# Rounded output projection, a fused norm guard and a band mask written one step ahead, in a six-layer local-attention kernel

## The chip, the cores and the metric

The kernel runs on one core of one Trainium2 chip. The metric is device time in microseconds: the median of three runs of the kernel before is 4177.26 us (4172.37 to 4178.75). The engines are named as in the profile: PE (TensorE, with PEld for its weight loads), DVE (VectorE), ACT (ScalarE), POOL (GpSimd) and SP (SyncE, which issues the DMAs).

## The reference

Eight sequences of 512 tokens, 128 channels. Stage 1 is a layer norm and one causal attention with 16 heads of 8 channels. Stage 2, where the change lies, is six layers, each an attention over a local window and a gated feed-forward. The attention of a layer:

```
qkv = shift_tokens(x) @ Wqkv               # 16 heads of 64 channels
q = l2norm(q) * q_scale; k = l2norm(k) * k_scale    # l2norm(t) = t / max(|t|, 1e-12)
q = q*cos*scale + rotate_half(q)*sin*scale ; k = k*cos/scale + rotate_half(k)*sin/scale
# window 32: each query sees its own window and the one before it,
# masked to keys j with j <= i <= j + 32
sim = einsum(q, k) * 8 ; sim = where(mask, -max, sim) ; attn = softmax(sim)
out = einsum(attn, v) @ Wo + x
```

## The kernel before

Activations lie channel by token. In stage 2 a layer is a loop over sequences `s` and eight steps `p` (`steps`, L674): a step works on one quad of heads (four heads, `QUADS = 4`) and one half of the tokens (`TOKS = 256`). The work is pipelined over steps. In step n each engine handles, in an order that is written out by hand:

- projection of q and k of step n (L1222 to L1224, into `proj_ps`), and of one tile of v (L1209 to L1211, into `vy_bank`);
- of step n-1 (`LAG_MIX`): the sum of squares per head (`same_head` matmul, L1198), its guard `max(ss, 1e-24)` on DVE (L1064), and ACT's Ln and Exp (L950, L953), which give the inverse norm;
- of step n-2 (`LAG_NORM`): `write_qk` on DVE (L783), rotated q and k times the inverse norm, one instruction of 1024 columns;
- of step n-3 (`LAG_SCORE`): the band mask (L1167: `ident_b` times `band_b`, bf16, which starts the accumulation in the two `score_bank`s), 128 small score matmuls of 32x32 tiles (L1177), the row maximum on DVE (L1020), the exponentials on ACT (L901, two halves of four), the inverse sums on DVE (L1027) and the normalising on POOL (L811);
- of step n-4 (`LAG_VALUE`): the transposes (L1157, into `tr_bank`), their copies on ACT and DVE (L891, L1047), the value products (L1246, 128x64 tiles, into `vy_bank`) and ACT's copy `y` (L943);
- of step n-5 (`LAG_WO`): the output projection in fp32 (L1259), two matmuls that the trace shows as four.

The steps are tied together by counting semaphores alone, and every engine runs its own queue in order. PE's order within a step is: mask, scores, transposes, sum of squares, v, projection of q and k, value products, output projection. DVE's: maxima, copy, `write_qk`, guard, inverse sum, inverse sum, and then the two products of the rotation (L1082 into `rotated`, L1087 into `by_sin`). ACT's: copy, four exponentials, copy of v (L924), four exponentials, square (L935), `y`, Ln, Exp. POOL's: the add of squares (L824), two rotations (L802), the two normalisations (L811). Step 3 also makes the rounded tokens of the next sequence (ACT L909, POOL L815 `tokens_rest`). In steps 5 to 7 stand the residual add and the layer norm of the sequence before (DVE L1033, L991, L996, L1002; ACT L868, L873, L875; PE `ffn_mean` and `ffn_var` at the end of steps 5 and 6). Behind the last sequence of a layer come six steps that drain the pipeline, and then the feed-forward.

"Rounded" values are the type fp32r: a matmul of it takes one pass where fp32 takes several; the products that need full accuracy are made of three such matmuls (high x high, high x rest, rest x high), as the projections here.

## Time and profile before

| | |
|---|---|
| median of 3 runs | 4177.26 us |
| the profiled execution's own time | 4182.92 us |
| its span (first to last instruction) | 4181.1 us |
| mean granted TensorE clock | 0.986 |
| PE busy | 3900.5 us (93%) |
| DVE busy | 3305.5 us (79%) |
| ACT busy | 3091.6 us (74%) |
| POOL busy | 2581.2 us (62%) |

Busy times are sums over the span. The span has stage 1 up to about 700 us, then six layers, each with 64 full steps, the draining steps, and the feed-forward. A row of the timeline gives the start of an operation in microseconds from the span's start, its duration, engine, line, what it writes and reads, how many neighbours it merges, and the idle time before it with what ended it.

### The profile page before, as it was taken

The page shows a single profiled execution, that of the slowest core. Times are in us where ns is not written, and L with a number is a line of the kernel's source. Part 1 is how long each engine was busy: PE and PEld are TensorE (multiplying, and loading weights), DVE is VectorE, ACT ScalarE, POOL GpSimd, SP SyncE. Part 2 cuts the span into 40 slices and gives each one's busy share as a digit, 9 for nine tenths or more (in the row PEclk, how much of TensorE's full clock was granted, in tenths as well). Part 3 has the DMA queues.
Part 4 walks back from the last instruction along what each step waited for, and adds up shares of the span by engine and source line. Part 5 has one row for each costly group of instructions (what it writes and reads, how often), then busy time and mean ns, then how long its engine had stood idle before and what let it go on. Part 6 is the DMA issues. An engine that isn't in the chain of part 4 may idle for free.

```text
span 4181.1 us, 190344 instructions
## 1 busy us (share of the span) xinstructions
PE 3900.5 (93%) x78816; PEld 3039.7 (73%) x78816; DVE 3305.5 (79%) x5294; ACT 3091.6 (74%) x10376; POOL 2581.2 (62%) x2583
## 2 busy tenths in 40 slices
PE   6888885999998999989999989999899999899998
PEld 3555554888866888848888668888488887588884
DVE  6778874988866888938888668989489886698894
ACT  5877785888865888838888658888488886588883
POOL 4667765766645676627666456766377664566660
PEclk9999998999999999999999999999999999999999
DMA  1000001111111111111111111111111111111110
GB/s 35 2 2 2 2 2 53 47 45 45 46 56 38 45 47 45 44 50 44 49 44 46 58 36 47 44 49 42 53 44 47 47 44 61 35 45 46 47 43 26
DMA packets 100195, 167.40 MB, mean 40 GB/s; under 512 B 26224, under 2 KB 33648, under 8 KB 99056
## 3 DMA queue, kind: packets, MB, share of 16 engines
q1 hardware_dynamic: 99312, 154.89, 12.6%
q8 instruction: 644, 10.55, 1.1%
q14 instruction: 239, 1.96, 0.2%
HBM read 26.13 MB, written 2.10 MB: 7 GB/s over the span
## 4 chain that ended last, share of the span: by engine, by line
PE 69%; issue 9%; POOL 3%; DVE 1%; ACT 0%; DMA 0%; SPq 0%; POOLq 0%; DVEq 0%; ACTq 0%
PE s_bank L1177 13%; PE s_bank L1246 10%; PE s_bank L1259 9%; PE s_bank L1198 8%; PE s_bank L1157 5%; PE s_proj L1222 4%; PE s_proj L1223 4%; PE s_proj L1224 4%; PE s_bank L1209 2%; PE s_bank L1210 2%; PE s_bank L1211 2%; PE s_bank L1167 2%; PE s_bank L1140 1%; POOL s_rotated L802 1%; PE s_bank L1289 1%
## 5 line engine op out<-in xcount | busy, mean ns | idle before, releaser
L802 POOL TENSOR_TENSOR s_rotated<-s_rotated,s_by_sin 128x512 f32<-128x512 f32 x768 | 983.8, 1302 | 227.3 <-DVE s_by_sin L1087 225.2
L811 POOL TENSOR_TENSOR s_probs<-s_probs,s_rden 128x256 f32<-128x256 f32 x768 | 479.7, 641 | 729.8 <-DVE s_rden L1027 729.3
L901 ACT ACTIVATE s_probs<-s_bank,s_neg_max 128x64 f32<-128x64 f32 x3072 | 908.0, 310 | 5.7 <-DVE s_neg_max L1020 5.6
L783 DVE TENSOR_TENSOR s_qk<-s_rotated,s_inv_norm 128x1024 f32<-128x1024 f32 x384 | 743.8, 1937 | 11.5
L1082 DVE TENSOR_TENSOR s_rotated<-s_proj,s_cos 128x1024 f32<-128x1024 f32 x384 | 469.6, 1223 | 241.5 <-ACT s_sq L935 240.9
L901 ACT ACTIVATION_READ_ACCUMULATOR s_probs<-s_bank,s_neg_max 128x1 f32 x3072 | 636.1, 207 | 0.0
L891 ACT ACTIVATE s_probs_t<-s_bank 64x512 f32<-64x512 f32 x384 | 226.8, 591 | 524.8 <-PE s_bank L1157 524.8
L1177 PE MATMUL s_bank<-s_qk 32*32 32x64 f32 x49152 | 581.4, 223 | 26.3 <-issue 25.9
L1177 PEld LDWEIGHTS s_bank<-s_qk 32*32 32x32 f32 x49152 | 510.9, 103 | 115.4 <-issue 114.6
L213 POOL TENSOR_TENSOR s_probs<-s_probs,s_rden 128x384 f32<-128x384 f32 (+3 forms) x512 | 406.4, 802 | 206.1 <-DVE s_rden L406 202.2
L824 POOL TENSOR_TENSOR s_sq<-s_sq 128x512 f32<-128x512 f32 x384 | 490.2, 1277 | 65.5 <-ACT s_sq L935 59.8
L1087 DVE TENSOR_TENSOR s_by_sin<-s_proj,s_sin 128x1024 f32<-128x1024 f32 x384 | 466.2, 1214 | 0.0
L1246 PE MATMUL s_bank<-s_probs_t,s_v 128*64 128x64 f32 x12288 | 445.5, 226 | 21.8 <-ACT s_probs_t L891 17.1
L1246 PEld LDWEIGHTS s_bank<-s_probs_t,s_v 128*64 128x64 f32 x12288 | 393.0, 138 | 77.1 <-ACT s_probs_t L891 21.4
L1198 PE MATMUL s_bank<-s_sq,s_same_head 128*128 128x256 f32 x1536 | 403.9, 386 | 40.2 <-POOL s_sq L824 37.9
L1222 PE MATMUL s_proj<-s_xs_high,s_w_high 128*128 128x256 f32 x1536 | 437.1, 285 | 0.0
L1259 PE MATMUL s_bank<-s_y,s_wo 128*128 128x256 f32 x1536 | 436.9, 407 | 0.0
L1223 PE MATMUL s_proj<-s_xs_rest,s_w_high 128*128 128x256 f32 x1536 | 436.6, 284 | 0.0
L1224 PE MATMUL s_proj<-s_xs_high,s_w_rest 128*128 128x256 f32 x1536 | 435.2, 283 | 0.0
L935 ACT ACTIVATE s_sq<-s_proj 128x1024 f32<-128x1024 f32 x384 | 397.8, 1036 | 25.2 <-PE s_proj L1224 25.2
L1020 DVE TENSOR_REDUCE s_neg_max<-s_bank 128x4 f32<-128x256 f32 x768 | 289.0, 418 | 72.1 <-PE s_bank L1177 69.1
L295 ACT ACTIVATE s_probs<-s_bank,s_neg_max 128x384 f32<-128x384 f32 (+3 forms) x512 | 271.9, 533 | 89.3 <-DVE s_neg_max L397 85.7
(118 smaller groups left out, 8156.2 us busy)
## 6 DMA issues: line engine op xcount, KB each, us to landing
s_v<-s_v SPq DMA_DIRECT2D x384, 192.0 KB, 2.5
s_v<-s_v SPq DMA_DIRECT2D x384, 64.0 KB, 2.4
s_qk<-f_wqk SPq DMA_DIRECT2D x6, 1024.0 KB, 6.4
s_xs_raw<-u SPq DMA_DIRECT2D x48, 128.0 KB
s_xf<-u SPq DMA_DIRECT2D x48, 128.0 KB, 2.3
s_xs_raw<-u SPq DMA_DIRECT2D x48, 127.8 KB
s_xf<-u SPq DMA_DIRECT2D x48, 127.8 KB, 2.6
s_qk<-f_wv SPq DMA_DIRECT2D x6, 512.0 KB, 6.8
```

The costliest lines, as they stand in the source:

```text
L783: return nc.vector.tensor_tensor(qk[:, quad % 2, :, :, at:at + TOKS], rotated[:, par, :, :, :], by, ALU.mult)
L802: nc.gpsimd.tensor_tensor(rotated[:, par, :, half, :], rotated[:, par, :, half, :], by_sin[:, :, 1 - half, :], (ALU.subtract, ALU.add)[half])\
L811: nc.gpsimd.tensor_tensor(part, part, by, ALU.mult).then_inc(S["probs_done"], 1)
L824: nc.gpsimd.tensor_tensor(sq[:, :, 0, :], sq[:, :, 0, :], sq[:, :, 1, :], ALU.add)\
L901: last = nc.scalar.activation(probs[:, par, h, b, :], score_bank[h][:, b * KEYS:(b + 1) * KEYS], ACT.Exp, scale=-1.0, bias=neg_max[:, par, ...
L1177: last = nc.tensor.matmul(score_bank[e][to:to + WIN, w * KEYS:(w + 1) * KEYS], qk[rows, quad % 2, 0, c, WIN + at:WIN + at + WIN], qk[rows, ...
L1198: last = nc.tensor.matmul(ss_bank[:, i * TOKS:(i + 1) * TOKS], same_head[:, :], sq[:, i, 0, :], start=True, stop=True)
L1222: nc.tensor.matmul(proj_ps[:, i, c, :], w[0], xs_high[:, s % 2, at:at + TOKS], start=True, stop=False)
L1223: nc.tensor.matmul(proj_ps[:, i, c, :], w[0], xs_rest[:, s % 2, at:at + TOKS], start=False, stop=False)
L1224: last = nc.tensor.matmul(proj_ps[:, i, c, :], w[1], xs_high[:, s % 2, at:at + TOKS], start=False, stop=True)
L1246: last = nc.tensor.matmul(mixed[HD * h:HD * (h + 1), pair, t, :, e, :], v[:, cols, (half * NT + t) * 2 + e, at:at + HD], probs_t[:, e, t, ...
L1259: last = nc.tensor.matmul(wo_bank[:, half * TOKS:(half + 1) * TOKS], wo[:, 2 * quad + pair, :], y[:, par, pair, :], start=(p == LAG_WO and ...
```

## The change

1. Output projection: `Wo` is loaded with the other weights and split into a high and a rest part; `y` is rounded by ACT to `y_high`, DVE subtracts to get `y_rest`, and PE makes three fp32r matmuls per pair of heads instead of one fp32 matmul. DVE's subtraction stands behind `inverse_sum(0)`, PE waits for it (`y_rest`).
2. The value products have their own bank `y_bank`. The v projection goes to `tr_bank`; its copy on ACT moves behind the square.
3. PE's order: scores, transposes, sum of squares, projection of q and k, v, output projection, mask for the next step's scores, value products.
4. The mask is fp32r instead of bf16, and is written one step ahead. The waits for `norm_done` and `exp_done` stand before it.
5. The guard on DVE goes. ACT's Ln reads the bank directly with a bias (`log_floor`), and `write_qk` takes the minimum with 1e12 in the same instruction as the product, in two instructions of 512 columns.
6. The waits on `guard_done` become waits on `log_done`; `ffn_mean` and `ffn_var` wait for it too.

The core of the diff:

```diff
-                                 (w_raw[:, QUADS * 4 * P // SEQ:, :], in_rows(of_layer("f_wv"))),
-                                 (wo[:, :, :].rearrange("p a n -> p (a n)"), of_layer("f_wo")),
+                                 (w_raw[:, QUADS * 4 * P // SEQ:(QUADS * 4 * P + INNER) // SEQ, :], in_rows(of_layer("f_wv"))),
+                                 (w_raw[:, (QUADS * 4 * P + INNER) // SEQ:, :], in_rows(of_layer("f_wo"))),
...
-            by = inv_norm[:, par, :, :].unsqueeze(2).to_broadcast([P, 2, 2, TOKS])
-            return nc.vector.tensor_tensor(qk[:, quad % 2, :, :, at:at + TOKS], rotated[:, par, :, :, :], by, ALU.mult)
+            for i in range(2):
+                by = inv_norm[:, par, i, :].unsqueeze(1).to_broadcast([P, 2, TOKS])
+                last = nc.vector.scalar_tensor_tensor(qk[:, quad % 2, i, :, at:at + TOKS], by, NORM_CUT,
+                                                      rotated[:, par, i, :, :], ALU.min, ALU.mult)
+            return last
...
-                    act.wait_ge(S["v_mm"], n + 1)
-                    nc.scalar.activation(v[:, p // TILES, 2 * (p % TILES), :], vy_bank[:, :], ACT.Copy)\
-                      .then_inc(S["v_done"], 1)
...
+                    act.wait_ge(S["v_mm"], n + 1)
+                    nc.scalar.activation(v[:, p // TILES, 2 * (p % TILES), :], tr_bank[:, :], ACT.Copy)\
+                      .then_inc(S["v_done"], 1)
+                if live(s, p, LAG_MIX, first):
+
+                    m, par = n - LAG_MIX, place(p, LAG_MIX)[2]
+                    act.wait_ge(S["ss_done"], m + 1)
+                    if not (first and p < LAG_MIX + 2):
+                        act.wait_ge(S["norm_done"], m - 1)
+                    nc.scalar.activation(inv_norm[:, par, :, :].rearrange("p a t -> p (a t)"), ss_bank[:, :], ACT.Ln,
+                                         scale=LN_SCALE, bias=log_floor[:, 0:1]).then_inc(S["log_done"], 1)
...
-                    act.wait_ge(S["guard_done"], m + 1)
-                    nc.scalar.activation(inv_norm[:, par, :, :], inv_norm[:, par, :, :], ACT.Ln, scale=LN_SCALE)\
-                      .then_inc(S["log_done"], 1)
...
-                if live(s, p, LAG_MIX, first):
-                    m, par = n - LAG_MIX, place(p, LAG_MIX)[2]
-                    dve.wait_ge(S["ss_done"], m + 1)
-
-                    if not (first and p < LAG_MIX + 2):
-                        dve.wait_ge(S["norm_done"], m - 1)
-                    nc.vector.tensor_scalar(inv_norm[:, par, :, :].rearrange("p a t -> p (a t)"), ss_bank[:, :],
-                                            NORM_FLOOR, None, ALU.max).then_inc(S["guard_done"], 1)
                 if score:
                     inverse_sum(0)
+                if live(s, p, LAG_WO, first):
+                    m, par = n - LAG_WO, place(p, LAG_WO)[2]
+                    dve.wait_ge(S["y_done"], m + 1)
+                    nc.vector.tensor_tensor(y_rest[:, par, :, :], y_bank[:, :].rearrange("p (a t) -> p a t", a=2),
+                                            y_high[:, par, :, :].bitcast(F32), ALU.subtract).then_inc(S["y_rest"], 1)
...
+                if full:
+                    if live(s, p, LAG_VALUE, first):
+                        pe.wait_ge(S["pt_first"], n - LAG_VALUE + 1)
+                        pe.wait_ge(S["pt_second"], n - LAG_VALUE + 1)
+                    if not (first and p == 0):
+                        pe.wait_ge(S["v_done"], n)
+                    toks, cols = slice(p % TILES * P, (p % TILES + 1) * P), slice(p // TILES * (INNER // 2), (p // TILES + 1) * (INNER // 2))
+                    nc.tensor.matmul(tr_bank[:, :], xs_high[:, s % 2, toks], wv[0][:, cols], start=True, stop=False)
+                    nc.tensor.matmul(tr_bank[:, :], xs_high[:, s % 2, toks], wv[1][:, cols], start=False, stop=False)
+                    nc.tensor.matmul(tr_bank[:, :], xs_rest[:, s % 2, toks], wv[0][:, cols], start=False, stop=True)\
+                      .then_inc(S["v_mm"], 1)
+                if live(s, p, LAG_WO, first):
+                    m = n - LAG_WO
+                    quad, half, par = place(p, LAG_WO)
+                    pe.wait_ge(S["y_done"], m + 1)
+                    pe.wait_ge(S["y_rest"], m + 1)
+                    if p == LAG_WO and not first:
+                        pe.wait_ge(S["attn_res"], l * NSEQ + s)
+                    for pair in range(2):
+                        into, w = wo_bank[:, half * TOKS:(half + 1) * TOKS], [part[:, 2 * quad + pair, :] for part in wo]
+                        nc.tensor.matmul(into, w[0], y_high[:, par, pair, :], start=(p == LAG_WO and pair == 0),
+                                         stop=False, skip_group_check=True)
+                        nc.tensor.matmul(into, w[0], y_rest[:, par, pair, :], start=False, stop=False, skip_group_check=True)
+                        last = nc.tensor.matmul(into, w[1], y_high[:, par, pair, :], start=False,
+                                                stop=(quad == QUADS - 1 and pair == 1), skip_group_check=True)
+                    last.then_inc(S["wo_done"], 1)
+                if live(s, p, LAG_SCORE - 1, first):
+
+                    half = place(p, LAG_SCORE - 1)[1]
+
+                    pe.wait_ge(S["norm_done"], n + 1 - LAG_SCORE + 1)
+                    if not (first and p == LAG_SCORE - 1):
+                        pe.wait_ge(S["exp_done"], 2 * (n - LAG_SCORE) + 2)
+                    for e in range(2):
+                        nc.tensor.matmul(score_bank[e][:, 0:NW * KEYS], ident_r[:, :], band_r[:, 1 if half or e else 0, :],
+                                         start=True, stop=False, skip_group_check=True)
```

## Rows read from the trace of the kernel before

**Rows 1.** The page, its part on busy time: us, share of the span, instructions.

```profile
PE 3900.5 (93%) x78816; PEld 3039.7 (73%) x78816; DVE 3305.5 (79%) x5294; ACT 3091.6 (74%) x10376; POOL 2581.2 (62%) x2583
```

**Rows 2.** PE's timeline of one regular step (step 2 of a sequence, third layer).

```profile
1937.13 1.48 PE L1177 MATMUL s_bank<-s_qk 32*32 32x64 f32 x128
...
1939.03 1.03 PE L1198 MATMUL s_bank<-s_sq,s_same_head 128*128 128x256 f32 x4
1939.71 0.58 PE L1209 MATMUL s_bank<-s_w_high,s_xs_high 128*128 128x512 f32 x1
...
1940.60 0.28 PE L1222 MATMUL s_proj<-s_xs_high,s_w_high 128*128 128x256 f32 x1
...
1942.10 1.15 PE L1246 MATMUL s_bank<-s_probs_t,s_v 128*64 128x64 f32 x32
1943.18 1.13 PE L1259 MATMUL s_bank<-s_y,s_wo 128*128 128x256 f32 x4
1944.15 0.38 PE L1167 MATMUL s_bank<-s_band_b,s_ident_b 128*128 128x256 bf16 x2
1944.46 1.48 PE L1177 MATMUL s_bank<-s_qk 32*32 32x64 f32 x128
```

**Rows 3.** DVE's timeline of the same step and the next `write_qk`.

```profile
1940.09 2.27 DVE L783 TENSOR_TENSOR s_qk<-s_rotated,s_inv_norm 128x1024 f32<-128x1024 f32 x1
1942.39 0.69 DVE L1064 TENSOR_SCALAR s_inv_norm<-s_bank 128x512 f32<-128x512 f32 x1
1943.00 0.23 DVE L1027 RECIPROCAL s_rden<-s_den 128x4 f32<-128x4 f32 x2
1943.64 1.23 DVE L1082 TENSOR_TENSOR s_rotated<-s_proj,s_cos 128x1024 f32<-128x1024 f32 x1 [0.41 <-ACT s_sq L935]
1944.78 1.22 DVE L1087 TENSOR_TENSOR s_by_sin<-s_proj,s_sin 128x1024 f32<-128x1024 f32 x1
...
1947.42 2.26 DVE L783 TENSOR_TENSOR s_qk<-s_rotated,s_inv_norm 128x1024 f32<-128x1024 f32 x1
```

**Rows 4.** A DVE copy and the PE row that waited for it, from a draining step.

```profile
2362.36 0.69 DVE L1047 COPY s_probs_t<-s_bank 64x512 f32<-64x512 f32 x1
```

**Rows 5.** The PE row that belongs to it.

```profile
2363.15 1.15 PE L1246 MATMUL s_bank<-s_probs_t,s_v 128*64 128x64 f32 x32 [0.96 <-ACT s_probs_t L891]
```

**Rows 6.** PE's timeline: two fp32r matmuls behind an idle stretch, at a layer's start.

```profile
1288.06 0.49 PE L1209 MATMUL s_bank<-s_w_high,s_xs_high 128*128 128x512 f32 x1 [1.69 <-issue]
...
1288.39 0.40 PE L1210 MATMUL s_bank<-s_w_rest,s_xs_high 128*128 128x512 f32 x1
```

**Rows 7.** ACT's timeline of the same step as rows 2.

```profile
1939.29 0.59 ACT L891 ACTIVATE s_probs_t<-s_bank 64x512 f32<-64x512 f32 x1 [1.25 <-PE s_bank L1157]
...
1940.94 0.59 ACT L924 ACTIVATE s_v<-s_bank 128x512 f32<-128x512 f32 x1
1941.42 0.31 ACT L901 ACTIVATE s_probs<-s_bank,s_neg_max 128x64 f32<-128x64 f32 x1
...
1942.57 1.03 ACT L935 ACTIVATE s_sq<-s_proj 128x1024 f32<-128x1024 f32 x1
```

**Rows 8.** POOL's timeline of the same step and the next (step 3, with `tokens_rest`).

```profile
1938.75 2.53 POOL L802 TENSOR_TENSOR s_rotated<-s_rotated,s_by_sin 128x512 f32<-128x512 f32 x2 [0.58 <-DVE s_by_sin L1087]
...
1946.08 2.53 POOL L802 TENSOR_TENSOR s_rotated<-s_rotated,s_by_sin 128x512 f32<-128x512 f32 x2 [0.41 <-DVE s_by_sin L1087]
1948.56 2.33 POOL L815 TENSOR_TENSOR s_xs_rest<-s_xs_raw,s_xs_high 128x544 fp32r<-128x544 f32 x1
```

**Rows 9.** Single lines over the whole span: ns minimum/median/maximum.

```profile
L783 DVE TENSOR_TENSOR s_qk<-s_rotated,s_inv_norm x384: 1215/2113/2340, 724.3 to 4090.6; 128x1024 f32<-128x1024 f32 x192
...
L996 DVE TENSOR_TENSOR s_xc<-s_xc,s_rstd x48: 659/660/1386, 824.6 to 4129.4; 128x512 f32<-128x512 f32 x48
...
L1008 DVE SCALAR_TENSOR_TENSOR s_v<-s_bank,s_vec,s_v x96: 734/747/753, 1226.4 to 4163.5; 128x512 f32<-128x512 f32 x48, 85x512 f32<-85x512 f32 x48
```

**Rows 10.** The waits: who waited, us in total, times, longest.

```profile
PEld s_bank L1177 <- issue: 114.6, 431, 2.5
```

More of the change, by code:

```diff
@@ L661, in build_stage2 @@
         names = ("const_in consts cast zeroed attn_w ffn_w tables w_high w_rest xs_in xs_high xs_rest proj_done sq_done sqadd_done prod_done "
-                 "add_done ss_done guard_done log_done inv_done norm_done score_done max_done exp_done "
-                 "rden_done probs_done tr_done pt_first pt_second v_mm v_done v_moved0 v_moved1 v_moved2 v_moved3 pv_done y_done wo_done attn_res "
+                 "add_done ss_done log_done inv_done norm_done score_done max_done exp_done "
+                 "rden_done probs_done tr_done pt_first pt_second v_mm v_done v_moved0 v_moved1 v_moved2 v_moved3 pv_done y_done y_rest wo_done attn_res "
                  "xf_in f_mean f_xc f_sq f_var f_log f_rstd f_xn f_xa f_up f_gate f_hid f_down ffn_res "
@@ L1162, in step @@
                     quad, half, par = place(p, LAG_SCORE)
-                    pe.wait_ge(S["norm_done"], m + 1)
-                    if not (first and p == LAG_SCORE):
-                        pe.wait_ge(S["exp_done"], 2 * m)
-                    for e in range(2):
-                        nc.tensor.matmul(score_bank[e][:, 0:NW * KEYS], ident_b[:, :], band_b[:, 1 if half or e else 0, :],
-                                         start=True, stop=False, skip_group_check=True)
                     for w in range(NW):
@@ L1203, in step @@
                         pe.wait_ge(S["xs_rest"], l * NSEQ + s + 1)
-                    if not (first and p < LAG_VALUE + 1):
-                        pe.wait_ge(S["y_done"], n - LAG_VALUE)
-                    if not (first and p == 0):
-                        pe.wait_ge(S["v_done"], n)
-                    toks, cols = slice(p % TILES * P, (p % TILES + 1) * P), slice(p // TILES * (INNER // 2), (p // TILES + 1) * (INNER // 2))
-                    nc.tensor.matmul(vy_bank[:, :], xs_high[:, s % 2, toks], wv[0][:, cols], start=True, stop=False)
-                    nc.tensor.matmul(vy_bank[:, :], xs_high[:, s % 2, toks], wv[1][:, cols], start=False, stop=False)
-                    nc.tensor.matmul(vy_bank[:, :], xs_rest[:, s % 2, toks], wv[0][:, cols], start=False, stop=True)\
-                      .then_inc(S["v_mm"], 1)
-                if full:
                     if not (first and p == 0):
@@ L1251, in step @@
                     last.then_inc(S["pv_done"], 1)
-                if live(s, p, LAG_WO, first):
-                    m = n - LAG_WO
-                    quad, half, par = place(p, LAG_WO)
-                    pe.wait_ge(S["y_done"], m + 1)
-                    if p == LAG_WO and not first:
-                        pe.wait_ge(S["attn_res"], l * NSEQ + s)
-                    for pair in range(2):
-                        last = nc.tensor.matmul(wo_bank[:, half * TOKS:(half + 1) * TOKS], wo[:, 2 * quad + pair, :],
-                                                y[:, par, pair, :], start=(p == LAG_WO and pair == 0),
-                                                stop=(quad == QUADS - 1 and pair == 1), skip_group_check=True)
-                    last.then_inc(S["wo_done"], 1)
                 if s == NSEQ and p == 0:
```

52 lines of the change are left out of this document (27 added, 25 removed).

## The prediction

> **What bounds the kernel now.** I read the page first. PE is busy 93% of the span, far above the others [rows 1]. Busy time alone doesn't say that PE sets the pace, so I read the timeline of one regular step, engine by engine. PE's rows follow each other without a gap from one block of scores (1937.13) to the next (1944.46) [rows 2]: a step takes 7.33 us, and PE waits for nobody. DVE idles 0.41 us before L1082 [rows 3], ACT 1.25 us before L891 [rows 7]. So a regular step is bound by PE, and the question is whether the other engines still arrive in time when PE's order changes. All times below count from the first score matmul of a step.
>
> **What PE saves.** Now the output projection takes 0.97 us from its start to the mask, and the mask 0.31 us to the scores [rows 2]. The 12 fp32r matmuls of the projection take 1.50 us up to the value products, 0.12 each with about 0.1 for the change of tile shape behind them [rows 2]. Six such for the output projection are 0.72, two for the mask 0.24. Projections (q and k, then v) stay 15 matmuls; the last ends at 4.97 - 0.1 = 4.87. Then 0.72 + 0.24 + 0.1 + 1.08 (value products) + 0.1 (change to the 32x32 tiles; no row shows this pair, 0 to 0.2, I take the change that I know) = 2.24. PE's own work is 7.11 us a step, 0.22 less.
>
> A rule stands for this side of the change: the Trainium skill (TensorEngine Tiling (Array Packing), Key Properties) says that changing the tiling mode drains TensorE. The new order has three such changes a step where there were four. By that rule nothing more than the 0.1 that is already in the sum is gained.
>
> **What PE must now wait for.** The output projection wants `y_rest` at 4.87. DVE makes it in the same step, in order, behind both halves of `write_qk` and one inverse sum. `write_qk` starts at 1940.09 - 1937.13 = 2.96 and nothing before it changes. Its own cost is not in the trace: two SCALAR_TENSOR_TENSOR of 512 columns. From below it is the 1.22 of the undisturbed single instruction; a plain product of 512 columns takes 0.66, and a SCALAR_TENSOR_TENSOR of 512 that reads PSUM 0.75 [rows 9], so at most 2 x 0.75 = 1.5. Two neighbours overlap by 0.08 (the copy 1942.39 + 0.69 ends at 1943.08, the next starts at 1943.00 [rows 3]). I take 1.37, so the earliest end is W = 4.33. Behind it 0.03 and about 0.07 of the inverse sum, then `y_rest`, 512 columns out of PSUM like the guard, 0.69: ends at W + 0.79. PE's value products start 0.10 us behind the DVE copy that they waited for (2362.36 + 0.69 = 2363.05 against 2363.15) [rows 4, 5]. After an idle stretch the first 512-column matmul takes 0.33 us to the next where it needs 0.23 [rows 6], so 0.10 more (0 to 0.2). From there to the next scores 2.24. Together T = W + 0.79 + 0.10 + 0.11 + 2.24 = W + 3.24. **With the earliest W that is 7.57, against 7.33 now.** The stall of 0.36 at the least eats the 0.22 saved.
>
> **What makes W later.** `write_qk` took 2.27 us here, its minimum 1.22 [rows 9]. POOL's two rotations end at 1938.75 + 2.53 = 1941.28 and `write_qk` ends at 1942.36, 1.08 later; in the next step 1948.61 and 1949.68, again 1.07 [rows 3, 8]. DVE makes next to no progress while POOL has a two-input operation from SBUF going: W = end of the rotations + 1.08 + 0.15 for the two instructions, if that is over 4.33. The Trainium skill (VectorE: DVE Perf Modes, Two Vector instructions with no wait between them) has the second SBUF read interface shared with GpSimd; the rows agree, and the new instructions still read two SBUF tensors, so by the rule the split frees nothing.
>
> The rotations start 0.07 behind L1087 (1937.46 + 1.22, then 1938.75). L1087 hangs on ACT's square. ACT: copy at 2.16, exponentials from 2.66, two halves of 1.15 (1941.42 to 1942.57 [rows 7]) now without the copy of v between them, square at 4.96 to 5.99. DVE: L1082 at 6.03, L1087 at 7.17 to 8.39. In the next step that is R = 8.39 - T, the rotations end at R + 2.60 and W = R + 3.82. Then T + T' = 8.39 + 3.82 + 3.24 = 15.45: two neighbouring steps alternate between 7.57 and 7.88, mean 7.72.
>
> **Over a sequence**, against 7.33 (the layer-norm matmuls behind steps 5 and 6 stay and are in neither number):
> - steps 1, 4, 7 at the floor: +0.24 each; step 2 and step 5: +0.55 each; step 6: +0.34 (floor, and 0.1 for `ffn_var`, which now waits for ACT's Ln).
> - step 0: step 7 puts two 512-column operations of the layer norm (0.66 [rows 9], less overlap) between `y_rest` (5.12) and L1082, which comes at 6.38 instead of 6.03; then R = 1.17, W = 4.99, T = 8.23: +0.90.
> - step 3: POOL's `tokens_rest` (L815) starts when the rotations end. Now it takes 2.33 us, of which DVE has the port for 1.1 [rows 8, 3]; it needs about 1.2 alone. With `write_qk` in two pieces I expect it to go in between: W = 3.1 + 0.6 + 1.2 + 0.7 = 5.6, T = 8.84: +1.51.
>
> Sum +4.57 a sequence; 42 sequences have all of it: +192. The first ones of the layers have five such steps each: 30 x 0.4 = +12. PE's irregular halts ("issue", 114.6 us [rows 10]) fall partly into slack that a waiting PE has: -15. The weights to split are 1024 columns longer, once in the open at the start, on ACT and on DVE, 1.0 us each by L935 (1024 columns in 1.03 [rows 7]): +2. Draining steps: output projection and mask 0.2 cheaper, `y_rest` newly in the chain: -5 to +15, I take +2. Behind the other layers the splitting lies under the feed-forward. Total +193. The profiled execution took 4182.92 us; its own forecast is 4376. It lies 5.7 above the median of the runs, and against that median it is **4370 us**.
>
> What costs nothing: the guard that goes is replaced one for one by `y_rest` (0.69 both); the copy of v (0.59) lands in ACT at 5.9, before the value products end, where ACT had 1.25 us to spare. The mask's two waits: `norm_done` at W, `exp_done` at 5.0, both earlier than the mask at W + 1.7. If the stall of `y_rest` were gone, `exp_done` at 5.0 against 5.59 would still be in time.
>
> **The rivals.**
> - *The port is left alone at step 3* (DVE keeps it through both halves, as L815 had to wait now): step 3 costs +0.55, its successors a little more; 1.0 x 42 less: about 4330. For it: L815 waited through all of `write_qk` [rows 8]. Against: that was one instruction.
> - *The new instructions don't wait for POOL*, every step is at the floor: (8 x 0.24 + 0.1) x 42 + 7 - 5 = about +87: 4265. Against: the 1.08 repeats to 0.01.
> - *`y_rest` is in time, PE's saving stands* (the other side). It would need W at 4.87 - 0.89 = 3.98, so `write_qk` within 1.02 us of its start; then 0.22 x 366 steps = -80: 4095. Against: the shortest of 384 took 1.215 us [rows 9]. Only if DVE started it earlier than 2.96 could it be so. At W = 4.09 it breaks even.
> - *The price of the wait is as above, but the fp32r matmuls cost more* (weight loads between them): six at 0.2 instead of 0.12, T 0.5 more: above 4450.
>
> **How the numbers follow.** Forecast 0.45, port left alone 0.30, floor 0.12, saving stands 0.06, a balance near nothing 0.03, more than 4460 0.04. The range leaves out the last three: 4250 to 4460. About 0.2% (8 us) is what a measurement here can tell from no change. Faster 0.06, same 0.03, slower 0.91.
>
> **What would show it.** PE idle before the first matmul of the output projection, released by DVE's `y_rest`, 0.3 to 1.1 us in nearly every full step, some 200 us together. Step periods of 7.57 in pairs with 7.9, one near 8.8 at step 3 and near 8.2 at step 0. The second half of `write_qk` stretched at step 3. ACT's square starting at 4.96. I am wrong if PE's rows follow each other without a gap as now, or if the largest wait of PE is one for `norm_done` or `log_done`.

## The result, and the profile after

The changed kernel takes **4493.68 us** (median of 4 runs, 4490.08 to 4499.95), the kernel before took 4174.82 (4 runs, 4170.65 to 4178.75). The ratio is 1.0766 (95% interval 1.0747 to 1.0784). The forecast was 4370 with a range up to 4460: the direction is right, but of 319 us lost only 193 had been foreseen. The profiled execution took 4490.35 us, with a span of 4488.6 and a mean granted clock of 0.985 (before: 0.986), so the clock is not the cause.

The page of the kernel after, busy time, then the instruction queue of the DMA (packets, MB, share), then the engines of the chain that ended last:

```profile
PE 3931.6 (88%) x79584; PEld 3052.5 (68%) x79584; DVE 3228.5 (72%) x5678; ACT 3114.3 (69%) x10376; POOL 2565.8 (57%) x2584
...
q8 instruction: 647, 10.60, 1.0%
...
PE 43%; DVE 18%; issue 15%; ACT 5%; POOL 3%; DVEq 0%; DMA 0%; SPq 0%; ACTq 0%; POOLq 0%
```

Against [rows 1] PE falls from 93% to 88% of a longer span: it has hardly more work (3931.6 us against 3900.5), it waits. DVE is now 18% of the chain, and "issue" (an engine waits for nothing that the profile shows) is 15%; in the kernel before these lines read as follows.

```profile
PE 69%; issue 9%; POOL 3%; DVE 1%; ACT 0%; DMA 0%; SPq 0%; POOLq 0%; DVEq 0%; ACTq 0%
```

The waits of the kernel after (who waited, for whom, us in total, times, longest):

```profile
PEld s_bank L1184 <- issue: 212.1, 252, 2.1
PE s_bank L1243 <- DVE s_y_rest L1078: 167.5, 267, 3.1
PE s_bank L1184 <- issue: 132.0, 169, 2.0
```

Two new waits stand on PE. One was forecast: the output projection (L1243) waits for `y_rest`. The other was not: within the score matmuls (L1184, before L1177) PE stands still 169 times, and the profile names nobody whom it waits for. Such a stop is called a halt below. Before, the weight loads had 114.6 us of it [rows 10] and the matmuls this:

```profile
PE s_bank L1177 <- issue: 25.9, 41, 2.3
```

Step 7 of a sequence (third layer), a step at the floor, PE and then DVE, ACT and POOL. It answers to [rows 2, 3, 7, 8].

```profile
2148.54 1.54 PE L1184 MATMUL s_bank<-s_qk 32*32 32x64 f32 x128
...
2153.78 0.36 PE L1243 MATMUL s_bank<-s_y_high,s_w_high 128*128 128x256 f32 x1
...
2154.55 0.39 PE L1257 MATMUL s_bank<-s_band_r,s_ident_r 128*128 128x256 f32 x2
2154.87 1.15 PE L1276 MATMUL s_bank<-s_probs_t,s_v 128*64 128x64 f32 x32
2155.95 0.28 PE L1184 MATMUL s_bank<-s_qk 32*32 32x64 f32 x7
```

```profile
2151.53 1.29 DVE L791 SCALAR_TENSOR_TENSOR s_qk<-s_inv_norm,s_rotated 128x512 f32<-128x512 f32 x2
2152.74 0.17 DVE L1042 RECIPROCAL s_rden<-s_den 128x4 f32<-128x4 f32 x1
2152.94 0.69 DVE L1078 TENSOR_TENSOR s_y_rest<-s_bank,s_y_high 128x512 fp32r<-128x512 f32 x1
```

```profile
2153.60 1.03 ACT L941 ACTIVATE s_sq<-s_proj 128x1024 f32<-128x1024 f32 x1
```

```profile
2148.84 2.50 POOL L813 TENSOR_TENSOR s_rotated<-s_rotated,s_by_sin 128x512 f32<-128x512 f32 x2 [1.11 <-DVE s_by_sin L1099]
```

The step takes 2155.95 - 2148.54 = 7.41 (forecast 7.57). `write_qk` ends at 4.28 (4.33), `y_rest` at 5.09 (5.12), the projection starts at 5.24 (5.22), ACT's square at 5.06 (4.96).

Step 3 of the next sequence, with both losses in it, PE first, then DVE and POOL:

```profile
2181.11 1.00 PE L1184 MATMUL s_bank<-s_qk 32*32 32x64 f32 x77
2182.64 0.74 PE L1184 MATMUL s_bank<-s_qk 32*32 32x64 f32 x51 [0.52 <-issue]
...
2187.68 0.35 PE L1243 MATMUL s_bank<-s_y_high,s_w_high 128*128 128x256 f32 x1 [0.72 <-DVE s_y_rest L1078]
...
2189.87 0.57 PE L1184 MATMUL s_bank<-s_qk 32*32 32x64 f32 x35
```

```profile
2184.86 1.86 DVE L791 SCALAR_TENSOR_TENSOR s_qk<-s_inv_norm,s_rotated 128x512 f32<-128x512 f32 x2
...
2186.84 0.69 DVE L1078 TENSOR_TENSOR s_y_rest<-s_bank,s_y_high 128x512 fp32r<-128x512 f32 x1
```

```profile
2181.76 2.49 POOL L813 TENSOR_TENSOR s_rotated<-s_rotated,s_by_sin 128x512 f32<-128x512 f32 x2 [0.95 <-DVE s_by_sin L1099]
2184.22 1.35 POOL L826 TENSOR_TENSOR s_xs_rest<-s_xs_raw,s_xs_high 128x544 fp32r<-128x544 f32 x1
```

The score matmuls stop after 77 of 128 with no releaser named. POOL's L826 takes 1.35 us in place of 2.33 [rows 8]. The halt had made DVE late: L826 started 0.64 us ahead of `write_qk`, ran through, and held both halves up, which end at 5.61 (forecast 5.6). The step takes 8.76 (forecast 8.84).

In a step 3 without a halt (third layer, fifth sequence, scores from 2248.45) L826 starts behind the first half, and the second half is held up:

```profile
2251.43 2.88 DVE L791 SCALAR_TENSOR_TENSOR s_qk<-s_inv_norm,s_rotated 128x512 f32<-128x512 f32 x2
```

```profile
2251.96 1.80 POOL L826 TENSOR_TENSOR s_xs_rest<-s_xs_raw,s_xs_high 128x544 fp32r<-128x544 f32 x1
```

Here `write_qk` ends at 5.86. Of the 36 inner steps 3 with a `tokens_rest`, 18 have a halt (median period 8.75) and 18 have none (9.03). In steps 0 it is 8.48 with a halt and 8.47 without. In these two steps, where the wait for `y_rest` is long, a halt costs little; in step 1 it costs 1 us (about 8.9 with, 7.84 without).

Means of the step periods over the 42 inner sequences (all but the first of each layer), from the starts of the score matmuls (us):

| step | 0 | 1 | 2 | 3 | 4 | 5 | 6 | 7 | sum |
|---|---|---|---|---|---|---|---|---|---|
| before | 7.44 | 7.66 | 7.41 | 7.40 | 7.45 | 8.51 | 8.22 | 7.35 | 61.43 |
| after | 8.50 | 8.47 | 8.11 | 8.83 | 8.21 | 9.25 | 8.96 | 7.51 | 67.84 |
| after, 10th percentile | 8.46 | 7.83 | 7.83 | 8.29 | 7.40 | 8.84 | 8.68 | 7.39 | |

42 sequences x 6.41 = 269 of the 307 us between the two profiled spans. Most of the rest is in the draining steps: the two step periods at the end of each layer add up to 121.9 us in the six layers, before to 80.0. There PE has no projections between the sum of squares and the output projection, and the wait for `y_rest` stands open (the end of the third layer):

```profile
2501.56 0.36 PE L1243 MATMUL s_bank<-s_y_high,s_w_high 128*128 128x256 f32 x1 [2.31 <-DVE s_y_rest L1078]
...
2510.86 0.36 PE L1243 MATMUL s_bank<-s_y_high,s_w_high 128*128 128x256 f32 x1 [3.14 <-DVE s_y_rest L1078]
...
2512.58 1.98 PE L1276 MATMUL s_bank<-s_probs_t,s_v 128*64 128x64 f32 x32
```

Behind the wait of 3.14 us the granted clock is 0.54 from 2510.9 to 2514.4, the lower of TensorE's two levels (1.2 of 2.4 GHz), after 1.00 from 2507.0 to 2510.7, in which PE was busy for 0.71 us. The value products take 1.90 us to the scores there, elsewhere 1.08.

Back to the inner steps: the means of steps 1, 4 and 5 are 0.4 to 0.8 above their own low values. So something irregular comes on top of the regular stall. Three theories were tested:
- **Stall**: the halts in the scores are a consequence of PE having waited; without the wait for `y_rest` they go.
- **Collision**: the large moves of `v` (192 KB, issued by SP when the value products start) now land in the scores and hold something up.
- **Burst**: the value products (64 instructions: 32 matmuls, each with its weight load) now stand directly in front of the scores (256 instructions). 320 short instructions follow each other in 2.5 us, and PE runs out of instructions to execute.

### The profile page after: what moved, and what is told of

It reads as the page before. It is cut to its first block, busy times and chain, and to the rows that moved or that the text cites. A ratio compares the mean times of both kernels' runs of the same rounds, so it can differ in the third digit from the quotient of the medians.

```text
span 4488.6 us, 191983 instructions
## 1 busy us (share of the span) xinstructions
PE 3931.6 (88%) x79584; PEld 3052.5 (68%) x79584; DVE 3228.5 (72%) x5678; ACT 3114.3 (69%) x10376; POOL 2565.8 (57%) x2584
## 4 chain that ended last, share of the span: by engine, by line
PE 43%; DVE 18%; issue 15%; ACT 5%; POOL 3%; DVEq 0%; DMA 0%; SPq 0%; ACTq 0%; POOLq 0%
PE s_bank L1184 12%; DVE s_qk L791 9%; PE s_bank L1276 8%; DVE s_y_rest L1078 4%; DVE s_neg_max L1035 3%; PE s_bank L1243 3%; ACT s_probs L912 3%; PE s_bank L1152 2%; PE s_bank L1170 2%; PE s_bank L1205 2%; PE s_bank L1246 2%; PE s_bank L1245 2%; PE s_bank L1257 2%; PE s_bank L1308 1%; PE s_bank L1146 1%
## 5 line engine op out<-in xcount | busy, mean ns | idle before, releaser
L813 POOL TENSOR_TENSOR s_rotated<-s_rotated,s_by_sin 128x512 f32<-128x512 f32 x768 | 970.0, 1284 | 375.3 <-DVE s_by_sin L1099 374.8
L1184 PE MATMUL s_bank<-s_qk 32*32 32x64 f32 x49152 | 618.0, 224 | 132.3 <-issue 132.0
L1184 PEld LDWEIGHTS s_bank<-s_qk 32*32 32x32 f32 x49152 | 527.0, 103 | 234.5 <-issue 212.1
L791 DVE SCALAR_TENSOR_TENSOR s_qk<-s_inv_norm,s_rotated 128x512 f32<-128x512 f32 x768 | 609.6, 834 | 11.5
L1218 PE MATMUL s_proj<-s_xs_high,s_w_high 128*128 128x256 f32 x1536 | 503.9, 328 | 46.2 <-POOL s_xs_rest L826 31.0
L835 POOL TENSOR_TENSOR s_sq<-s_sq 128x512 f32<-128x512 f32 x384 | 500.0, 1302 | 53.6 <-ACT s_sq L941 37.9
L1099 DVE TENSOR_TENSOR s_by_sin<-s_proj,s_sin 128x1024 f32<-128x1024 f32 x384 | 465.9, 1213 | 0.0
L1276 PE MATMUL s_bank<-s_probs_t,s_v 128*64 128x64 f32 x12288 | 456.6, 229 | 0.0
L961 ACT ACTIVATE s_y_high<-s_bank 128x512 fp32r<-128x512 f32 x384 | 229.3, 597 | 306.8 <-PE s_bank L1276 306.8
L1276 PEld LDWEIGHTS s_bank<-s_probs_t,s_v 128*64 128x64 f32 x12288 | 402.9, 142 | 51.9 <-issue 3.3
L1243 PE MATMUL s_bank<-s_y_high,s_w_high 128*128 128x256 f32 x768 | 247.3, 322 | 180.7 <-DVE s_y_rest L1078 167.5
```

The source lines that it names most:

```text
L791: last = nc.vector.scalar_tensor_tensor(qk[:, quad % 2, i, :, at:at + TOKS], by, NORM_CUT, rotated[:, par, i, :, :], ALU.min, ALU.mult)
L813: nc.gpsimd.tensor_tensor(rotated[:, par, :, half, :], rotated[:, par, :, half, :], by_sin[:, :, 1 - half, :], (ALU.subtract, ALU.add)[half])\
L835: nc.gpsimd.tensor_tensor(sq[:, :, 0, :], sq[:, :, 0, :], sq[:, :, 1, :], ALU.add)\
L1099: nc.vector.tensor_tensor(by_sin[:, :, :, :], proj_ps[:, :, :, :], rot_sin[:, :, :, toks], ALU.mult).then_inc(S["prod_done"], 1)
L1184: last = nc.tensor.matmul(score_bank[e][to:to + WIN, w * KEYS:(w + 1) * KEYS], qk[rows, quad % 2, 0, c, WIN + at:WIN + at + WIN], qk[rows, ...
L1218: nc.tensor.matmul(proj_ps[:, i, c, :], w[0], xs_high[:, s % 2, at:at + TOKS], start=True, stop=False)
```

## The experiments

Every kernel was timed beside the kernel before on the same chip; the chips of the different rounds differ by up to 14 us in the kernel before, so a few us between rounds say nothing; each has its own kernel before beside it. "Wait in the scores" is the row of PE for "issue" at the score line.

**e1: `y_rest` early.** DVE makes `y_rest` ahead of `write_qk`; only its place on DVE moves.

```diff
+                if live(s, p, LAG_WO, first):
+                    m, par = n - LAG_WO, place(p, LAG_WO)[2]
+                    dve.wait_ge(S["y_done"], m + 1)
+                    nc.vector.tensor_tensor(y_rest[:, par, :, :], y_bank[:, :].rearrange("p (a t) -> p a t", a=2),
...
                 if norm:
...
-                if live(s, p, LAG_WO, first):
-                    m, par = n - LAG_WO, place(p, LAG_WO)[2]
-                    dve.wait_ge(S["y_done"], m + 1)
-                    nc.vector.tensor_tensor(y_rest[:, par, :, :], y_bank[:, :].rearrange("p (a t) -> p a t", a=2),
...
```

> The changed kernel with DVE's y_rest moved in front of write_qk, all else as it is. Wait theory (the prediction's): PE's wait for y_rest goes, a regular step falls to PE's own 7.1 us. Three theories for the halts inside the score matmuls (PE idle put down to issue there: 132 us in the changed kernel, 26 before). Burst theory: value products directly in front of the scores are 64 + 256 instructions in 2.5 us, more than the supply of instructions gives; the order is untouched here, so the halts stay, about 4215 us (4180 to 4280). Stall theory: PE's stop for y_rest is what starves it afterwards; the halts go with the stop, about 4090. Collision theory (the moves of the values by DMA now fall onto the scores and slow the fetching of instructions): halts stay, 4215.

Measured: 4315.59 us (4310.85 to 4319.15) against 4180.42; ratio 1.0315 (1.0294 to 1.0336). The waits of e1:

```profile
PEld s_bank L1184 <- issue: 234.3, 233, 2.5
PE s_bank L1184 <- issue: 159.8, 152, 2.4
...
PE s_bank L1243 <- DVE s_y_rest L1068: 35.9, 24, 1.7
```

The time is above the expected range (4180 to 4280). The wait for `y_rest` falls from 167.5 to 35.9 us and the kernel gains 178. The halts in the scores stay and grow from 132.0 to 159.8: **the stall theory falls**. What is left of the loss, 135 us, comes without a stall. PE's timeline of one such halt in e1:

```profile
1120.64 1.15 PE L1276 MATMUL s_bank<-s_probs_t,s_v 128*64 128x64 f32 x32
1121.73 1.15 PE L1184 MATMUL s_bank<-s_qk 32*32 32x64 f32 x94
1123.67 0.53 PE L1184 MATMUL s_bank<-s_qk 32*32 32x64 f32 x34 [0.79 <-issue]
```

and the DMA's view of the 0.2 us from 1121.2 on, in which one packet of the instruction queue starts (packets, MB, share of 16 engines):

```profile
q8 instruction: 1, 0.02, 29.0%
```

**e2: value products first.** In PE's order they stand in front of the output projection and the mask, in place of behind them, and wait for `y_rest` (they write the bank that it reads).

```diff
-                if live(s, p, LAG_WO, first):
...
-                if live(s, p, LAG_SCORE - 1, first):
...
+                    if live(s, p, LAG_WO, first):
+                        pe.wait_ge(S["y_rest"], n - LAG_WO + 1)
...
                     last.then_inc(S["pv_done"], 1)
+                if live(s, p, LAG_WO, first):
...
+                if live(s, p, LAG_SCORE - 1, first):
...
```

> The changed kernel with PE's order values products, output projection, mask (instead of output projection, mask, value products); the value products wait for y_rest now, so the stop stays as long as it was, some 0.3 to 1 us a step. Burst theory: between the value products and the scores lie 1 us of long matmuls again, the halts in the scores fall from 132 us to 20 to 50 and the time by about 130, to 4360 (4320 to 4400). Stall theory and collision theory: unchanged, 4480 to 4500.

Measured: 4406.27 us against 4180.42; 1.0531 (1.0505 to 1.0558). The waits of e2:

```profile
PE s_bank L1253 <- DVE s_y_rest L1078: 201.7, 226, 3.4
PE s_bank L1184 <- issue: 54.0, 78, 1.7
```

The stall is there in full, the wait in the scores falls from 132.0 to 54.0 us. Both numbers lie just above what was expected (20 to 50 us, and a time up to 4400).

**e4: the new order alone, in the kernel before.** Nothing else of the change is in it: fp32 output projection, bf16 mask, guard, one `write_qk`, no `y_rest`. Only PE's order is the new one.

```diff
-                    pe.wait_ge(S["norm_done"], m + 1)
...
                     last.then_inc(S["proj_done"], 1)
+                if live(s, p, LAG_WO, first):
...
+                    last.then_inc(S["wo_done"], 1)
+                if live(s, p, LAG_SCORE - 1, first):
...
+                    pe.wait_ge(S["norm_done"], n + 1 - LAG_SCORE + 1)
+                    if not (first and p == LAG_SCORE - 1):
+                        pe.wait_ge(S["exp_done"], 2 * (n - LAG_SCORE) + 2)
+                    for e in range(2):
+                        nc.tensor.matmul(score_bank[e][:, 0:NW * KEYS], ident_b[:, :], band_b[:, 1 if half or e else 0, :],
+                                         start=True, stop=False, skip_group_check=True)
                 if live(s, p, LAG_VALUE, first):
...
                     last.then_inc(S["pv_done"], 1)
-                if live(s, p, LAG_WO, first):
...
```

> The kernel before with one part of the change: output projection (fp32 as it was) and mask (bf16, for the next step) moved in front of the value products, so that these stand directly before the scores. PE's own work is the same 7.33 us a step and nothing waits (norm_done at 5.2, exp_done at 5.5, the mask at 5.85). Burst theory: the halts come here too, about 4310 us (4260 to 4350) with over 100 us of issue in the scores. Stall theory: no stop for y_rest here, so 4175 as before. Collision theory: the moves of the values lie where they lay, 4175.

Measured: 4451.95 us against 4180.42; 1.0656 (1.0625 to 1.0688). The waits of e4, and one of its halts:

```profile
PEld s_bank L1171 <- issue: 338.4, 302, 2.3
...
PE s_bank L1171 <- issue: 236.2, 193, 2.2
```

```profile
1519.68 1.15 PE L1260 MATMUL s_bank<-s_probs_t,s_v 128*64 128x64 f32 x32
1520.76 0.84 PE L1171 MATMUL s_bank<-s_qk 32*32 32x64 f32 x63
1522.48 0.86 PE L1171 MATMUL s_bank<-s_qk 32*32 32x64 f32 x65 [0.89 <-issue]
```

This is the run that decides: **the order alone costs 271 us**, with no new wait for DVE. That is far above the 4260 to 4350 expected. "Nothing waits" was not quite right either: the mask, written ahead, now waits 40.2 us in all for ACT's exponentials (66 times), before 7.2. The rest goes with the halts. It also shows the good side of the order: steps without a halt take 7.15 where they took 7.34.

**e5: the moves of `v` later.** SP issues them only when the next scores are done.

```diff
+                    if not (s == 0 and p < 2):
+                        sp.wait_ge(S["score_done"], 2 * step_no(l, s, p) - 2)
```

> The changed kernel, but SP issues the moves of a step's values only when the scores of the next step are done, some 2 us later, so that they no longer run during the scores. Collision theory: the halts in the scores go, about 4360 us. Burst theory and stall theory: no change, 4480 to 4500, and the issue idle in the scores stays at about 130 us.

Measured: 4478.53 us against 4180.42; 1.0704 (1.0684 to 1.0724). The wait hardly changes (132.0 before this edit), so **the collision theory falls**; at most 15 us are its own. The trace says so too: during the scores the DMA queue of these moves keeps the 16 engines 35% busy in the kernel after, and 0% in e5, where 163 halts are left of 169.

```profile
PE s_bank L1186 <- issue: 127.1, 163, 1.4
```

**e3: both cures together** (the edits of e1 and e2).

> The changed kernel with both repairs: y_rest in front of write_qk on DVE, and PE's order value products, output projection, mask. Burst theory: nothing waits for y_rest and 1 us of long matmuls lies between the value products and the scores, so a regular step is near 7.1 us and the issue idle in the scores 30 to 80 us; about 4120 us (4090 to 4180), faster than the kernel before. If the halts had another cause that came with fp32r or with y_bank, they would stay above 100 us and the time near 4230.

Measured: 4152.19 us (4147.38 to 4161.44) against 4178.76; 0.9943 (0.9925 to 0.9961), 27 us faster than before.

```profile
PE s_bank L1184 <- issue: 10.8, 21, 1.1
```

The four kernels make a table of two by two (median us):

| | `y_rest` behind `write_qk` | `y_rest` ahead of it |
|---|---|---|
| value products in front of the scores | 4493.68 | 4315.59 |
| value products in front of the projection | 4406.27 | 4152.19 |

Down the columns the order is worth 87 and 163 us, along the rows the wait is worth 178 and 254. Together 341, less than 254 + 163 = 417: a halt and a stall of the same step partly cover each other, as in steps 0 and 3 above.

**e7: the v projection between the value products and the scores.** Three matmuls of 512 columns (0.7 us of PE's work in 6 instructions) should let the supply catch up.

```diff
-                if full:
...
-                    nc.tensor.matmul(tr_bank[:, :], xs_high[:, s % 2, toks], wv[0][:, cols], start=True, stop=False)
...
                     last.then_inc(S["pv_done"], 1)
+                if full:
...
+                    nc.tensor.matmul(tr_bank[:, :], xs_high[:, s % 2, toks], wv[0][:, cols], start=True, stop=False)
...
```

> The kernel with y_rest early (4316 us, 160 us of issue idle in the scores) and the v projection moved behind the value products, so that three 512-column matmuls (0.65 us, six instructions) lie between value products and scores; output projection and mask stay in front of the value products. Burst theory: the spacer alone is enough for most of it, issue idle falls to 50 to 100 us, time 4200 to 4260. If it were the place of mask or output projection that mattered, nothing would change: 4310 or, with one more change of tile shape, 4350.

Measured: 4508.89 us against 4178.76; 1.0794 (1.0776 to 1.0812). Not what was expected. The wait in the scores is halved (70.7 after 159.8), but the projection that is gone from its old place was the cover for the exponentials: the mask now waits for them in every step, and on ACT the copy of `v` waits 619.5 us.

```profile
PEld s_bank L1246 <- ACT s_probs L912: 177.6, 376, 2.2
...
PE s_bank L1184 <- issue: 70.7, 135, 1.6
```

The expected 4200 to 4260 was missed by far. Two things were changed at once, so the time decides nothing between the theories.

**e9: half of the value products in front.** Starting from e1, 32 of the 64 instructions stand in front of the output projection, 32 in front of the scores.

```diff
+                    for pair in range(1):
...
-                    for pair in range(2):
+                    for pair in range(1, 2):
```

> Dose test of the burst theory. The kernel with y_rest early (4316 us, 160 us of PE idle put down to issue in the scores), but half of the value products (pair 0) stands in front of output projection and mask and half behind: the burst before the end of the scores is 32 + 256 instructions instead of 64 + 256. Burst theory: idle in the scores falls to 80 to 120 us, which gives 50 to 80 us back; one more pair of changes of tile shape costs up to 0.17 x 378 = 64. Time 4250 to 4330. If the size of the burst doesn't matter, only that value products stand there, the idle stays at 150 to 170 and the time is 4330 to 4380.

Measured: 4314.25 us against 4188.49; 1.0297 (1.028 to 1.0314). The time is that of e1 (4315.59), but the wait in the scores is halved, as expected of the burst:

```profile
PE s_bank L1184 <- issue: 81.8, 126, 1.7
```

What the halts gave back went into the split: entering and leaving the value products' tile shape a second time costs 0.09 and 0.10 us a step, and two pieces of 16 take 0.615 us each where 32 in one take 1.08. Steps without a halt take 7.35 to 7.44 us in e9, 7.0 to 7.1 in e1.

**e11: half of the score matmuls.** From e1; the matmuls of the second half of the channels are left out, so that the burst is 64 + 128 instructions.

```diff
-                        for c in range(2):
+                        for c in range(1):
```

Measured: 3976.18 us against 4188.49; 0.949 (0.9474 to 0.9506). The halts are nearly gone (15 are left). The time lies 26 us above the expected range; the trace has a new wait that fits, for `write_qk`, since PE is too early now.

```profile
PE s_bank L1257 <- DVE s_qk L791: 68.5, 140, 1.3
...
PE s_bank L1184 <- issue: 9.9, 15, 1.1
```

**e6: one `write_qk`.** From the kernel after: one product in place of two instructions. It leaves out the minimum with 1e12.

```diff
-            for i in range(2):
...
-                last = nc.vector.scalar_tensor_tensor(qk[:, quad % 2, i, :, at:at + TOKS], by, NORM_CUT,
-                                                      rotated[:, par, i, :, :], ALU.min, ALU.mult)
...
+            return nc.vector.tensor_tensor(qk[:, quad % 2, :, :, at:at + TOKS], rotated[:, par, :, :, :], by, ALU.mult)
```

> The changed kernel with write_qk as one product of 1024 columns as before; it leaves out the minimum with 1e12. Port theory (tokens_rest on POOL slips in between the two halves at step 3 and holds the second up by about 1.2 us, and each half costs 0.07 more): about 50 us less, 4440 (4420 to 4465), and write_qk at step 3 is no longer stretched beyond the rotations' end + 1.1. If the split is free: 4494.

Measured: 4459.9 us against 4178.76; 1.0672 (1.0654 to 1.0689), 34 us less than the kernel after.

```profile
PE s_bank L1240 <- DVE s_y_rest L1075: 123.5, 129, 3.1
```

Step 3 falls from a mean of 8.83 to 8.31: 0.52 x 42 = 22 of the 34 us. All of it comes from the 18 steps 3 without a halt, in which POOL had slipped into the gap: there `write_qk` ends at 4.72 in place of 5.88, L823 (before L826) takes 2.33 us in place of 1.80, and the step 7.90 in place of 9.03. In the 18 with a halt, in which POOL starts first, nothing changes (5.60 and 5.61). The other steps had nothing to slip in; their floor falls from 7.40 to 7.33, since one product is cheaper than two instructions.

**e8: `tokens_rest` behind the normalising products on POOL**, from e3.

```diff
-                if p == XS_STEP and s < NSEQ - 1:
-                    tokens_rest(s + 1)
...
+                if p == XS_STEP and s < NSEQ - 1:
+                    tokens_rest(s + 1)
```

> The kernel with both repairs, and POOL's tokens_rest behind the two normalisations of step 3 instead of in front, where it can't slip between the halves of write_qk. In that kernel write_qk has slack before the mask, so the port theory expects little: 0 to 30 us less than the kernel with both repairs. If write_qk or what follows it were on the path there, 30 to 50 less.

Measured: 4151.95 us against 4178.76; 0.9939 (0.9923 to 0.9956), the time of e3. In step 3 `write_qk` ends at 4.94 in place of 6.09, and the step takes 7.28 us either way: with `y_rest` early nobody waits for `write_qk` there, so what slips between its halves costs nothing.

**e10: the best version.** From e3, ACT's Ln stands in front of the copy of `v`.

```diff
-                    act.wait_ge(S["v_mm"], n + 1)
-                    nc.scalar.activation(v[:, p // TILES, 2 * (p % TILES), :], tr_bank[:, :], ACT.Copy)\
...
                 if live(s, p, LAG_MIX, first):
...
+                if full:
+                    act.wait_ge(S["v_mm"], n + 1)
+                    nc.scalar.activation(v[:, p // TILES, 2 * (p % TILES), :], tr_bank[:, :], ACT.Copy)\
...
```

> A version for use: both repairs (4152 us), and ACT's Ln in front of the copy of v, so that ffn_mean and ffn_var at the ends of steps 5 and 6 need not wait for it. In the kernel with both repairs step 6 takes 8.68 us where its neighbours plus the layer-norm matmul make 8.14, step 5 8.31. Wait theory: 0.4 to 0.6 us a sequence come back, 42 times, so about 20 us less: 4130 (4115 to 4145). If the wait only moves to the transposes (they need the copy of v of the step before): unchanged, 4152.

Measured: **4138.23 us** (4126.25 to 4140.36) against 4188.49; 0.987 (0.9854 to 0.9887). It beats both kernels. Against the kernel before on its own chip that is 50 us, where e3 had 27; about 20 more had been expected. Step 6, in which `ffn_var` waits for the Ln, falls from a median of 8.68 to 8.21 us, step 5 from 8.31 to 8.14. A regular step of e10 takes 7.28 us.

## Why the prediction was right and where it was wrong

**The failed step** is the sentence "PE's irregular halts ("issue", 114.6 us [rows 10]) fall partly into slack that a waiting PE has: -15". It took the halts as given, to be covered better or worse. They depend on what stands in front of the scores, and the change altered exactly that. [Rows 2] showed the old order, value products, then the four matmuls of the output projection in 0.97 us, then the mask in 0.31, then the 128 score matmuls; the change takes these 1.28 us, in which PE needs 12 instructions, out from between two dense stretches. The prediction counted them as work moved from one place to another, at no cost. Summed over all gaps between score matmuls that are more than 0.1 us above the median one, the starts lag by 36 us in the kernel before, by 169 after, by 193 in e1, by 278 in e4 and by 16 in e3. In place of -15, the order costs 87 us net beside the late `y_rest` and 163 without it. One part of the sentence held: where PE waits long anyway, a halt is covered, as in steps 0 and 3. No rival had this mechanism.

**A second term was mis-sized**: "Draining steps: ... -5 to +15, I take +2". The draining steps and what follows them up to the next layer's scores take 34 us more (two step periods +42, the rest -8). With `y_rest` late alone (e2) the two periods add up to 121.7 us, with the order alone (e4) to 101.5, in e3 to 83.1, before to 80.0. So the wait for `y_rest`, which nothing covers there, is most of it.

**The sum, taken apart by the runs.** Of the 307 us between the profiled spans, 269 lie in the 42 inner sequences (forecast 192, less 15 for the halts), 7 in the first sequences of the layers (12), 34 at the layers' ends (2) and -3 ahead of the first scores (2). Of the times: before to e1 is +135, e1 to after +178 for `y_rest`, together 313 against 319 measured (the chips differ by 6 us in the kernel before). In the other order: before to e3 -27, e3 to e2 +254, e2 to after +87, together 314.

An estimate from the traces for the +135 of e1: steps without a halt take 7.09 instead of 7.34, -0.25 x 8 x 42 = -84; steps 5 and 6 take 8.33 and 8.69 where 8.18 - 0.25 would be left, since `ffn_mean` and `ffn_var` wait for the Ln, +49; the lag of the starts grows by 193 - 36 = 157; the mask waits 16.7 for `write_qk`. The sum is 139.

**PE's own work** was forecast at 7.11, it is 7.0 to 7.1. Of its terms, read in e1 (projection at 2083.91, mask at 2084.61, value products at 2084.94, scores at 2086.03): output projection 0.70 (forecast 0.72), mask with its change 0.33 (0.34), value products with the change to 32x32 tiles 1.09 (1.18). So fp32r was sized right. What was taken too high is the last change: from the start of the value products to what follows takes 1.08 us in the median, whether 128x128 matmuls follow (e3) or the scores (e1), so going on to the 32x32 tiles adds nothing to be seen. Between 128x128 matmuls the value products cost 0.09 us on the way in (v projection to what follows: 0.79 in e3, 0.70 in e1) and 0.10 on the way out (output projection 0.81 in e3, 0.71 in e1). The new order saves both: e3 is at 7.28 against e1's 7.08, and e4, which has no fp32r in these places, gets from 7.34 to 7.15. The Trainium skill (TensorEngine Tiling (Array Packing), Key Properties) says that a change of the tiling mode drains TensorE; the trace agrees in that these two changes cost 0.09 and 0.10 us, while the one from 128x64 to 32x32 shows no cost of its own.

**The wait for `y_rest`** was right in mechanism and size. T = W + 3.24 with W = 4.33: measured W 4.28, and 7.41 for the step, since the 3.24 is 3.13. The terms of the list, with PE's saving added back, are (4.57 + 8 x 0.22) x 42 + 12 = 278 us; e2 against e3, which measures that wait with few halts, gives 254, of which 39 are in the draining steps; e3's own step is 7.28 instead of the 7.11 that the 278 start from. The largest wait row was forecast at some 200 us and has 167.5.

**DVE's progress beside POOL** held in the steps 3 without a halt: `tokens_rest` slips between the halves, and `write_qk` ends at 5.88 in the median (5.6 forecast). The rival "port left alone" would have had it near 7.88 - 3.24 = 4.64; e6, which has no gap, has it at 4.72, so that rival was right for one instruction and wrong for two. In the steps 3 with a halt, as in the one shown first, POOL is ahead of both halves. That the 5.61 there meets the forecast of 5.6 is luck.

**Step 0** was forecast at 8.23: the median is 8.47. `write_qk` ends at 5.33 in place of 4.99. The second product of the rotation (L1099) starts 7.81 behind the scores of the step 7 shown, where the forecast's terms give 7.52, and that step is 0.16 shorter than the floor that was forecast. For both reasons the rotations come later in step 0.

**Step 6**, with its layer-norm matmuls, was forecast at 8.20 + 0.34 = 8.54: it is 8.68, since `ffn_var` waits longer for the Ln; e10 removes this by changing two operations on ACT.

**The rivals.** "`y_rest` in time", 4095, was refuted by the trace; but its mechanism is what e3 builds by moving `y_rest` (4152). "More than 4460" was given 0.04 for dearer fp32r matmuls; that was the right side for a wrong reason: they cost 0.12 each.

## What to carry to other kernels

Before reordering a tensor engine's work, count instructions as well as microseconds: a few long matmuls between two dense stretches of small ones can be the time in which the supply of instructions catches up, and taking them away can cost more than the reorder saves. The ends of a loop, where the pipeline drains, need a sum of their own: what hides a late operand in a full step may be missing there. A row "issue" ahead of the densest line, even a small one (25.9 us here), was a sign of it in this kernel's profile; it is worth a price of its own when the neighbours of that line change. An operand that arrives from another engine a few tenths too late is often cured by its place in that engine's order: ask which of its neighbours somebody waits for.

## What the runs showed of the hardware that was not expected

- **PE can run out of instructions.** The wait in the scores follows the number of instructions in the burst that ends in them: 64 + 256 gives 159.8 us (e1), 32 + 256 gives 81.8 (e9), 256 behind the output projection and mask 10.8 (e3) and 64 + 128 gives 9.9 (e11). That the burst causes the halts is shown by these runs. It isn't the only influence: e2 has the order of e3 and still 54.0 us, with the late `y_rest` as the only difference; why is open.
- **What PE waits for is the next packet of instructions.** The DMA's instruction queue q8 moved 10.55 MB in 644 packets of 16 KB in the kernel before; over 2 x 78816 instructions of PE that is at most 67 bytes for one. Count PE's instructions in order (weight loads, matmuls and its sequencer's own) from one halt in the scores to the next: in the kernel after it is a multiple of 256, give or take one, in 163 of 168 cases, and the other 5 are the changes of layer. It is so in all thirteen traces. 256 instructions in 16 KB are 64 bytes each. The scores, which are 256 instructions themselves, hold one such border in nearly every step; at 169 of the 384 borders PE halts in the kernel after, at 152 in e1, 193 in e4, 126 in e9, 41 before and 21 in e3. In every one of these halts PE resumes 2.2 to 3.3 us after the start of the last packet.
- **When the next packet is asked for stays open.** A step has 191 matmuls with as many loads, 382 instructions in 7.1 us or 54 a us; in the burst it is 320 in 2.5 us, 128 a us, so 256 of them pass in 2.0 us, less than the 2.2 from a packet's start to PE's going on. That fits, but no run changed the size or the time of the packets, and what starts a packet's move isn't in the traces.
- **A change of TensorE's tile shape** is priced by its neighbours: 0.09 us from 128x128 to 128x64, 0.10 back, nothing to be seen from 128x64 to 32x32 (medians of e1 and e3).
- **DVE's and POOL's two-operand instructions from SBUF hold each other up by whole instructions.** POOL's `tokens_rest` took 1.36 us where it started ahead of `write_qk`, 1.80 where it started within the first of two halves (the second half then took 1.84 in place of 0.68), and 2.33 beside one of 1024 columns [rows 8].
